# Attention rows grouped by head parity in a one-core transformer kernel, and the third attention rebuilt in the form of the first two

## The reference

```
x = patches @ W_lin + b; class token and positions added
h = global_latent_attn(norm(x))     # attention 1: 16 query heads of 16, 4 key/value heads, causal
h = local_gqa_attn(norm(h))         # attention 2: the same form, window 64 (all of 37 tokens)
h = h + moe(norm(h))                # 32 experts, 8 chosen per token, and 2 shared units
q, k, v = norm(h) @ qkv_w.T + qkv_b # attention 3: 16 heads of 16 each, not causal, biases
o = softmax(q k^T / 4) v            # per image and head
h = h + o @ out_w.T + out_b
out = h + ffn_int8(norm(h))         # two quantised linear layers
```

## Time and profile before

| | us |
|---|---|
| median of 3 runs (lowest, highest) | 389.59 (387.09, 391.3) |
| the profiled execution, and its span | 388.82, 386.7 |
| PE busy, share of span | 358.8, 93% |
| DVE busy | 232.7, 60% |
| ACT busy | 181.2, 47% |
| POOL busy | 140.7, 36% |

### The profile page before, as it was taken

The page is one execution under the profiler, slowest core; times in us unless marked ns, Lnnn a source line. Parts: engine busy times, 40 slices in busy tenths (PEclk is TensorE's granted clock), DMA queues, the critical chain, the costliest instruction groups (busy, mean ns, idle before and its releaser), DMA issues.

```text
span 386.7 us, 8832 instructions
## 1 busy us (share of the span) xinstructions
PE 358.8 (93%) x3419; PEld 302.0 (78%) x3419; DVE 232.7 (60%) x494; ACT 181.2 (47%) x373; POOL 140.7 (36%) x154
## 2 busy tenths in 40 slices
PE   8899889898999889999999999999999998999574
PEld 6555669566777879999999999999997666777342
DVE  0265686787759635555555555555554628845686
ACT  0156851386355324444444444444445467534171
POOL 0025841271250236666656544444320024500012
PEclk9999999999999989999999999999999999999899
DMA  8960000200450043444444444454300000000001
GB/s 296 350 222 0 3 4 8 102 3 3 163 166 3 9 158 91 146 139 144 142 140 144 138 144 143 144 144 144 104 0 3 0 2 2 3 3 0 2 1 63
DMA packets 14861, 33.58 MB, mean 87 GB/s; under 512 B 2480, under 2 KB 4464, under 8 KB 14320
## 3 DMA queue, kind: packets, MB, share of 16 engines
q1 hardware_dynamic: 12592, 31.23, 24.7%
q10 hardware_dynamic: 2240, 1.95, 1.5%
HBM read 32.49 MB, written 0.69 MB: 86 GB/s over the span
## 4 chain that ended last, share of the span: by engine, by line
PE 70%; DVE 16%; ACT 6%; DMA 4%; issue 3%; ACTq 1%; DVEq 0%
PE psum L1125 69%; DVE rc L886 3%; DMA region<-in_w_lin 2%; DVE xn L821 1%; DVE region L887 1%; ACT km L606 1%; DVE nt L815 1%; ACT region L778 1%; DMA wb<-weights 1%; DVE nt L818 1%; DVE nt L817 1%; DVE km L1107 1%; PE psum L1290 1%; DVE xc L806 1%; ACT region L687 1%
## 5 line engine op out<-in xcount | busy, mean ns | idle before, releaser
L1125 PE MATMUL psum<-xh,split_all 128*128 128x296 f32 x544 | 123.5, 301 | 1.9 <-DVE rt L1021 1.9
L1125 PEld LDWEIGHTS psum<-xh,split_all 128*128 128x128 f32 x544 | 92.7, 190 | 2.2 <-DVE rt L1021 2.2
L478 POOL TENSOR_TENSOR split_all<-km,split_all 128x768 fp32r<-128x768 f32 x34 | 63.2, 1863 | 85.0 <-ACT split_all L700 85.0
L1125 PE MATMUL psum<-xl,split_all 128*128 128x296 f32 (+1 forms) x288 | 85.6, 302 | 0.2 <-ACT e L667 0.2
L720 ACT ACTIVATE ah<-rt 128x296 fp32r<-128x296 f32 x68 | 30.8, 453 | 78.6 <-DVE rt L1021 72.1
L1125 PEld LDWEIGHTS psum<-xl,split_all 128*128 128x128 f32 (+1 forms) x288 | 53.7, 189 | 1.8 <-issue 1.1
L1023 DVE TENSOR_TENSOR al<-rt,ah 128x296 fp32r<-128x296 f32 x64 | 30.2, 472 | 33.2 <-ACT ah L720 33.2
L1125 PE MATMUL psum<-ah,split_all 128*128 128x296 f32 x272 | 48.5, 300 | 1.4 <-ACT ah L720 1.4
L1018 DVE TENSOR_TENSOR rb<-psum,wb 128x296 f32<-128x296 f32 x64 | 29.8, 466 | 32.7 <-ACT psum L718 29.0
L1125 PEld LDWEIGHTS psum<-ah,split_all 128*128 128x128 f32 x272 | 40.7, 188 | 1.8 <-ACT ah L720 1.8
L1021 DVE TENSOR_TENSOR rt<-rb,psum 128x296 f32<-128x296 f32 x64 | 29.6, 463 | 5.4 <-PE psum L1125 0.4
(11 more groups left out here) (174 smaller groups left out, 529.0 us busy)
## 6 DMA issues: line engine op xcount, KB each, us to landing
km<-in_experts SPq DMA_DIRECT2D x34, 384.0 KB, 4.0
wb<-weights SPq DMA_DIRECT2D x32, 296.0 KB, 3.7
w_sb<-in_w SPq DMA_DIRECT2D x2, 1024.0 KB, 11.8
region<-in_x SPq DMA_DIRECT2D x6, 296.0 KB, 5.3
region<-in_g_wo SPq DMA_DIRECT2D x1, 1024.0 KB, 4.8
region<-in_l_wo SPq DMA_DIRECT2D x1, 1024.0 KB, 4.9
region<-in_w_lin ACTq DMA_DIRECT2D x6, 128.0 KB, 6.7
qkv_sb<-in_qkv_w SPq DMA_DIRECT2D x1, 768.0 KB, 6.1
```

Source lines behind the costliest of these rows:

```text
L478: nc.gpsimd.tensor_tensor(wl[i], ring[i], wh[i].bitcast(f32), ALU.subtract)\
L1125: return nc.tensor.matmul(out_, lhsT, rhs, start=start, stop=stop, skip_group_check=True)
```

## The change

Rows of a score tile are now **one image's heads by parity**: block 0 of 64 rows holds the even query heads of each group, block 1 the odd ones, and the two images of a pair stand side by side along the columns. For this the columns of the query weights are permuted (`q_col`), and `v4` and `v16` hold each image's values in both row blocks. The outputs of an attention then lie as plain channels x tokens.

- Attentions 1 and 2: scores keep their 16 matmuls. Values take 8 matmuls of 74 columns per pair instead of 4 of 148, the sums still 4 of 148. The projection is dense: 8 matmuls of 296 columns, with an unpadded `wo_sb` (256 KB loaded instead of 1,024 KB, twice). The projection of the values is made for both row blocks, twice the work, in two halves: the second half stands in PE's order after the scores of the second pair (`value_sums(a, 1)`), and ACT copies it before its third exponential. `ATTENTION_BUSY` goes from 12 to 5. POOL clears `v4` (twice as wide) after its first scaling, no longer before.
- Attention 3: all masked copies are made before the loop, keys by DVE (16 of 296 columns), queries by ACT (16 of 296), into buffers that are free by then (`km`, `wb`, `x0`, `sq`). The diagonals move from DVE to POOL. PE runs `row_scores` two pairs ahead instead of one. `weighted_values` has the form of the first attentions: 16 matmuls of 32 rows and 37 columns and 4 with ones; DVE takes a reciprocal of 148 columns and writes `ot` directly. The transposes and ACT's output copies are gone. The value bias is multiplied with `out_w` once, by four matmuls of one column, and added to `out_b` (`outb`).

```diff
-ATTENTION_BUSY = 12
+ATTENTION_BUSY = 5
...
-        V4 = PAIRS * KVH * VP
-        OT = G4 * PAIRS * S
-        wo_sb = region[:, OT + V4:OT + V4 + 2 * G4 * D].rearrange("p (b g d) -> p b g d", b=2, g=G4)
+        V4 = B * KVH * VP
+        OT = C * T
+        wo_sb = region[:, OT + V4:OT + V4 + C * D].rearrange("p (c d) -> p c d", c=C)
...
+        wb_flat = wb[:].rearrange("p r t -> p (r t)")
+        qvar = [[z.rearrange("p (g t) -> p g t", g=4) for z in zs] for zs in
+                ([wb_flat[:, c * C * T:(c + 1) * C * T] for c in range(C)],
+                 [z[:].rearrange("p c t -> p (c t)") for z in (x0, sq)])]
...
@@ gpsimd: third attention
-            pool.wait_ge(s_qkev, 4)
             for p in range(PAIRS):
+                pool.wait_ge(s_mx, p + 1)
                 if p >= 2:
                     pool.wait_ge(s_s, 2 * PAIRS + p - 1)
-                for c in range(C):
-                    ins = variants(nc.gpsimd, qvar, qt, p, c)
-                    if c == C - 1:
-                        ins.then_inc(s_qvar, 1)
+                nc.gpsimd.tensor_tensor(dg[:, p % 2, :, :], mx[:, p % 2, :].unsqueeze(2).broadcast_to([P, HEADS, S]),
+                                        const("minus_ident").unsqueeze(1).broadcast_to([P, HEADS, S]), ALU.mult)\
+                    .then_inc(s_dg, 1)
...
@@ scalar
+            def last_query_variants(hf):
+
                 for c in range(C):
...
+                    for g in range(4):
+                        ins = nc.scalar.activation(qvar[hf][c][:, g, :], qt[:, c, half(hf)], ACT.Copy,
+                                                   scale=const("onehot4")[:, g:g + 1])
+                ins.then_inc(s_qvar, 1)
+
+            def values_copied(a, j):
+
+                act_e.wait_ge(s_vps, 2 * a + j + 1)
+                for g in range(2):
+                    rows = slice(64 * g, 64 * g + S)
+                    ins = nc.scalar.activation(v4[rows, HB * j:HB * (j + 1), :, g, :],
+                                               ps[2 + j][rows, :].rearrange("p (i h d) -> p i h d", i=HB, h=KVH),
+                                               ACT.Copy)
+                ins.then_inc(s_v, 1)
 
             def attention(a):
                 for p in range(PAIRS + 2):
-                    if a == 2 and p + 2 < PAIRS:
-                        last_key_variants(p + 2)
+                    if a < 2 and p == 2:
+                        values_copied(a, 1)
...
@@ vector
             def normalise_outputs(p):
+
                 n = 2 * PAIRS + p
                 dve.wait_ge(s_o, n + 1)
...
+                bank = ps[p % 2]
+                dve.wait_ge(s_on, n)
+                link(nc.vector.reciprocal(rc[:], bank[:, G4 * S:2 * G4 * S]))
+                nc.vector.tensor_tensor(ot[:, :, 2 * p * S:2 * (p + 1) * S].rearrange("p c (b s) -> p b c s", b=2),
+                                        bank[:, 0:G4 * S].rearrange("p (b c s) -> p b c s", b=2, c=C),
+                                        rc[:].rearrange("p (b c s) -> p b c s", b=2, c=C), ALU.mult).then_inc(s_on, 1)
...
+                dve.wait_ge(s_kev, 2 * hf + 2)
+                for c in range(C):
+                    for g in range(4):
+                        ins = nc.vector.tensor_scalar(kvar[:, c, g, half(hf)], kt[:, c, half(hf)],
+                                                      const("onehot4")[:, g:g + 1], None, ALU.mult)
+                ins.then_inc(s_kvar, 1)
             nc.vector.tensor_copy(pairs_r, const("pairs")).then_inc(s_kmr, 1)
-            dve.wait_ge(s_kev, 4)
-            for p in range(-1, PAIRS + 2):
-                if p + 1 < PAIRS:
-                    if p + 1 >= 2:
-                        dve.wait_ge(s_sq_s, p)
-                    variants(nc.vector, kvar, kt, p + 1, 0).then_inc(s_kvar, 1)
-                if 0 <= p < PAIRS:
+            dve.wait_ge(s_obias, 1)
+            nc.vector.tensor_tensor(outb[:], ps[3][:, 0:C], vector("out_b"), ALU.add).then_inc(s_obias, 1)
+            for p in range(PAIRS + 3):
+                if p < PAIRS:
                     dve.wait_ge(s_sq_s, p + 1)
+                    if p >= 2:
+                        dve.wait_ge(s_dg, p - 1)
                     nc.vector.tensor_reduce(
...
-                    nc.vector.tensor_tensor(dg[:, p % 2, :, :], bc(mx[:, p % 2, :].unsqueeze(2), [P, HEADS, S]),
-                                            bc(const("minus_ident").unsqueeze(1), [P, HEADS, S]), ALU.mult)\
-                        .then_inc(s_dg, 1)
-                if p >= 2:
-                    normalise_outputs(p - 2)
+                if p >= 3:
+                    normalise_outputs(p - 3)
...
@@ tensor
             def row_scores(p):
 
-                pe.wait_ge(s_kvar, p + 1)
-                pe.wait_ge(s_kvar1, p + 1)
+                pe.wait_ge(s_kvar, p // (PAIRS // 2) + 1)
                 if p >= 1:
                     pe.wait_ge(s_mx, p)
...
+                for b in range(2):
+                    at = (2 * p + b) * S
+                    for c in range(C):
+                        cols = slice((2 * b + c) * 2 * S, (2 * b + c + 1) * 2 * S)
+                        for r in range(2):
+                            rows = slice(64 * r, 64 * r + 64)
+                            for g in range(2):
+                                ins = mm(ps[4 + r][64 * g:64 * g + 64, cols].rearrange("p (v s) -> p v s", v=2),
+                                         qt[rows, c, at:at + 64], kvar[rows, c, g:4:2, at:at + S], True, True)
                 ins.then_inc(s_sq_s, 1)
...
             def grouped_values(a, p):
...
-                for part in range(2):
+                ex = e[0:ROWS, p % 2, 0:EC].rearrange("p (k b l n) -> p k b l n", k=2, b=2, l=2)
+                for b in range(2):
                     for kv in range(KVH):
...
+                        mm(ps[p % 2][VP * kv:VP * (kv + 1), b * C * S:(b + 1) * C * S],
+                           v4[0:ROWS, 2 * p + b, kv, :, :].rearrange("p g d -> p (g d)"),
+                           ex[:, kv // 2, b, kv % 2, :], True, True)
+                for kv in range(KVH):
+                    ins = mm(ps[p % 2][VP * kv:VP * (kv + 1), G4 * S:2 * G4 * S].rearrange("p (b n) -> p b n", b=2),
+                             const("pair_ones", ROWS), ex[:, kv // 2, :, kv % 2, :], True, True)
                 ins.then_inc(s_o, 1)
 
             def weighted_values(p):
...
-                for hd in range(HEADS):
-                    at = head_at(hd) * S
-                    rows = slice(64 * (hd % 2), 64 * (hd % 2) + EP)
-                    cols = slice(hd // 2 * 2 * (HD + 1), (hd // 2 + 1) * 2 * (HD + 1))
-                    ins = mm(ps[p % 2][rows, cols], e[0:ROWS, p % 2, at:at + EP],
-                             v16[0:ROWS, p, hd, :, :].rearrange("p b d -> p (b d)"), True, True)
+                ex = e[0:ROWS, p % 2, 0:EC].rearrange("p (r b c v n) -> p r b c v n", r=2, b=2, c=C, v=2)
+                for b in range(2):
+                    for c in range(C):
+                        for j in range(4):
+                            mm(ps[p % 2][VP * j:VP * (j + 1), (2 * b + c) * S:(2 * b + c + 1) * S],
+                               v16[0:ROWS, 2 * p + b, 4 * c + j, :, :].rearrange("p g d -> p (g d)"),
+                               ex[:, j // 2, b, c, j % 2, :], True, True)
+                for j in range(4):
+                    ins = mm(ps[p % 2][VP * j:VP * (j + 1), G4 * S:2 * G4 * S].rearrange("p (b c n) -> p b c n", b=2, c=C),
+                             const("pair_ones", ROWS), ex[:, j // 2, :, :, j % 2, :], True, True)
                 ins.then_inc(s_o, 1)
 
-            def transposes(p):
...
             def project_grouped(a):
 
-                N = HALF // 2
                 for hf in range(2):
                     pe.wait_ge(s_on, a * PAIRS + PAIRS // 2 * (hf + 1))
                     for m in range(C):
-                        for b in range(2):
-                            for g in range(G4):
-                                ins = mm(ps[4 + 2 * m + hf][:, b * N:(b + 1) * N], wo_sb[:, b, g, m * P:(m + 1) * P],
-                                         ot4[:, g, hf * N:(hf + 1) * N], g == 0, g == G4 - 1)
+                        for c in range(C):
+                            ins = mm(ps[4 + 2 * m + hf][:, 0:HALF], wo_sb[:, c, m * P:(m + 1) * P],
+                                     ot4[:, c, half(hf)], c == 0, c == C - 1)
                     ins.then_inc(s_wo, 1)
 
             def project_out():
                 for hf in range(2):
-                    pe.wait_ge(s_ot, 2 * (hf + 1))
+                    pe.wait_ge(s_on, 2 * PAIRS + PAIRS // 2 * (hf + 1))
...
             def attention(a):
-                lead = 1 if a == 2 else 0
-                for p in range(PAIRS + 2 + lead):
+                lead = 2 if a == 2 else 0
+                for p in range(PAIRS + 1 + lead):
...
                         if a < 2 and p == 1:
                             if a == 0:
```

(37 more changed lines are left out.)

190 lines of the change are left out of this document (57 added, 133 removed).

## The result

| | before | changed |
|---|---|---|
| median, us | 389.03 | 384.7 |
| lowest to highest (10 runs each) | 387.09 to 391.3 | 382.72 to 386.26 |
| profiled execution, its span | 388.82, 386.7 | 386.13, 384.3 |

The ratio is 0.9885 [0.9859, 0.9911]; by the medians the changed kernel is 4.3 us faster. The forecast was 9.1 us faster, 380.0. The time lies in the range and the direction is right, but the gain is just under half of what I forecast. The traces show that attentions 1 and 2 gave 5.7 us, 0.3 of them there before anything had changed, where the forecast had 6.3; attention 3 lost 1.5 where the forecast had a gain of 2.8. The two profiled executions are only 2.7 us apart, less than the medians, so the traces account for a smaller gain than the medians show.

The account below looks back on a forecast made before the run. DVE was taken to bound the loops of attentions 1 and 2, PE their projections and attention 3. Gains 3.1 (attention 1), 3.2 (attention 2) and 2.8 (attention 3) sum to 9.1 us: 380.0, range 376.0 to 386.0 (8 in 10).

Parts of the forecast that it names:

- Dense projection, attention 1: Projection after attention 1's loop: PE needs 4.15 us instead of 8.32, DVE then sets the pace; gain 3.1 us.
- Loops of attentions 1 and 2: Per pair, four more matmuls bring PE to 1.43 to 1.45 us, under DVE's 1.53; cost 0.
- the 1.6 that I had named as a sign of being wrong: Loops of attentions 1 and 2: forecast wrong if DVE's divisions stand over 1.6 us apart.
- Second value set: Second set of value matmuls: 2.0 us of PE in attention 2 where it waited 1.62; cost 0.3, in attention 1 0.
- Attention 3: First scores at 324.0, turns of 2.74 us instead of 3.20, end at 348.0 instead of 350.8; gain 2.8 us.
- 324.0 for the first scores: Start of attention 3: row scores start at 320.3, the first three wait for each other's maxima, first scores at 324.0.
- The clock rival: Attentions 1 and 2: TensorE's clock falls from 2.4 to 1.2 GHz until the projection's end, 14.3 us, hence 394.0; chance 0.04.
- a slice under 9: PE's granted clock: forecast wrong if any slice shows under 9.
- a turn over 3 us: Attention 3's loop: forecast wrong if a turn, put at 2.74 us, exceeds 3 us.
- Narrow matmuls at 33 ns: Values in all attentions and attention 3's row scores cost 33 ns a record: 8.0 us, hence 387.7, no change; chance 0.12.
- DVE as the bound: Attention 3: values take 0.25 us, PE's turn 2.39, DVE's 2.3 binds next; 377.0; chance 0.13.
- the fast rival: Attention 3: values at 0.25 us, eight turns 0.35 us shorter, 377.0; chance 0.13.

Follow-up runs that it names:

- more matmuls: Changed kernel with the matmuls that sum the exponentials split, 8 of 74 columns instead of 4 of 148 per pair in all three attentions: median 389.76 us, ratio 1.001.
- the last two kernels: Changed kernel with idle matmuls at two places and early bias product, float32 row scores: 383.31 us; with bf16 row scores and eight idle matmuls for six: 379.82 us.

## Why the prediction was half right

- **Dense projection, attention 1: right.** The next attention starts 71.96 - 68.28 = 3.68 us earlier, of which 0.29 was there before anything had changed (41.85 against 41.56). 3.4 measured, 3.1 forecast. DVE's second maximum follows its additions directly.
- **Loops of attentions 1 and 2: PE's price right, "cost 0" not quite.** PE's pair is 1.42 us and DVE's divisions stay 1.53 apart in attention 1. But attention 2's pairs have 60 records instead of 52, 128 in 3.27 us, and halts appear: 0.63 us in this trace, 1.0 to 1.9 in the others that kept those loops. Behind the three halts of this trace divisions stand 1.68 to 1.84 apart, over the 1.6 that I had named as a sign of being wrong.
- **Second value set: under-sized.** In attention 2 the lead falls from 3.68 to 91.44 - 88.30 = 3.14: 0.54, where I took 0.3. Attention 2 as a whole gave 2.0 us (5.70 at the router, where it was 3.68), not 3.2; halts and this make up most of the rest.
- **Attention 3: the step that failed.** I forecast 2.8 us and it lost 1.5. Its parts at full speed were mostly better than said: values 0.30 for 0.60 and a turn of 2.47 for 2.74, though the bias product was 1.0 for 0.8, as the row that I took it from had it (0.97 for eight records). I had counted a matmul's price in columns and in ns per record, and never asked how many instructions per microsecond that makes: 106 records per 2.47 us, 43 per us, against 21 before. That term was put at nothing, and the halts it brings cost 1.86 us of idle time and more by start times. And I had seen that the first row scores wait for each other's maxima, two pauses of 1 us, but priced only the pauses (324.0 for the first scores) and not the clock behind them, 2.1 us.
- **The clock rival stood at the wrong place.** I had put it in attentions 1 and 2 at 14 us and 0.04; it came for 6.8 us at the start of attention 3, cost 2.1, and I had named a slice under 9 as a sign that I am wrong, as I had a turn over 3 us (3.12 with the first gap). So it was. Another fall, over the first quantised products, lasted 6.8 us where the kernel before had one of 3.4, and took about 1 us more of the lead.
- **Narrow matmuls at 33 ns, and DVE as the bound: neither.** In four tiles 37 columns cost 0.30 / 32 = 9 ns. That is the fast rival's premise (values at 0.25), but its turn of 2.39 us and its 377.0 did not come: 1.77 + 0.30 + 0.40 is 2.47, and the halts and the clock stand on top.
- **The Trainium skill.** "TensorE: Matmul & The Clock Gate", section "Wait — 56ns, not 53.3ns?", has a floor of about 25 ns from start to start. For 8 columns with 128 x 128 weights the trace agrees (26 ns, at either clock); for 32 weight columns in four column groups it does not (9 ns). "Runtime: NRT & Kernel Launch", section "Instruction fetch mechanics", says that crossing a 16 KiB boundary of 256 instructions is mostly hidden. That holds for the kernel before (no gap) and not for the changed one: 2.5 us, and 9.1 with more matmuls.

From the end of one halt to the end of the next PE issued 126 or 127 records, in 3.33 us (from 94.99 in the changed kernel) up to 4.07 us (from 329.71). Both stretches are made of two parts: from the end of the halt until the next packet starts (1.1 and 1.8 us), and from there until PE goes on (2.2 and 2.3 us). Open: why a packet starts sooner or later after a halt, and whether pauses alone bring the clock down, since once they did not.

## What to carry to other kernels

Count the matmuls per microsecond as well as their columns: above some 38 records per us, kept up over a few hundred, PE waited for its own instructions here, and what a smaller tile saves in columns comes back as "issue". When a change brings a new wait into PE's stream, look for the clock behind it: the half clock cost as much here as the pauses themselves (2.1 us beside two of 1 us), and in the five traces with idle matmuls in the pauses it did not fall. A value that only steers can be bf16: 16 records a pair instead of 32, and 3.5 us of the time between the last two kernels.

## What the runs showed of the hardware

- Issue gaps depend on the count of matmuls and not on columns: 0, 2.5 and 9.1 us in the span for 52, 60 and 68 records a pair (with the row scores and values of attention 3 going the same way).
- Every gap ended 2.2 to 3.0 us after a 16 KB packet of instructions had started, 70 gaps in 11 traces. In the loops the next packet started 1.0 to 1.8 us after the gap's end.
- A train of 8-column matmuls kept its 26 ns per record when the granted clock fell from 1.00 to 0.50 (records that touch a window of 0.4 us, at 348.8 and 350.0):

```profile
348.80:349.20 0.40, 0.40 (x22) 1.00 0.00 0
...
350.00:350.40 0.40, 0.40 (x21) 0.50 0.00 0
```

PE had issued such matmuls without a pause when the clock fell.
